# Third mixer cut into slices behind the edge sum of the third graph layer, on one core

## What is computed

```python
xn = _layernorm(x, axis=-1)
x = x + _L3_gnn_ref(xn, ...) + _L3_mix_ref(xn[None], ...)[0]
```

```python
q, k, v = x @ Wq, x @ Wk, x @ Wv           # 8 heads
Q, K = elu(q) + 1, elu(k) + 1
msg = Q (K^T v) / (Q sum(K))                # per head
msg = _layernorm(msg @ Wm, g1, b1)
h = relu(concatenate([x, msg], axis=-1) @ W1) @ W2
return x + _layernorm(h, g2, b2)
```

## Time and profile before

| | us |
|---|---|
| median of the 3 runs | 9672.11 |
| the profiled execution: its time | 9659.98 |
| the profiled execution: its span | 9658.3 |
| third graph layer, 6966 to 8807 | 1841 |
| in it, the stage of `state_scan`, 7468 to 8327 | 859 |
| third mixer, 8807 to 9190 | 383 |

### The profile page before, as it was taken

One profiled execution on the slowest core, in us unless ns is written; L12 is line 12 of the kernel. 1 busy time (PEld: TensorE's weight loads), 2 busy tenths in 40 slices (PEclk: granted clock), 3 DMA queues, 4 the chain that ended last, 5 costly groups with the idle time before them and its releaser, 6 DMA issues. The chain is left out here.

```text
span 9658.3 us, 89308 instructions
## 1 busy us (share of the span) xinstructions
PE 6492.2 (67%) x25974; PEld 4040.2 (42%) x25974; DVE 5133.1 (53%) x10543; ACT 2741.6 (28%) x6163; POOL 3646.3 (38%) x3646
## 2 busy tenths in 40 slices
PE   6848587799577556479965645655843777547766
PEld 6824233344455434347743333433441333223344
DVE  7832475323788654621067555455664888543221
ACT  0112100222355133112224432331233555233311
POOL 2635577001277367230054745750120555110111
PEclk5569656899799766679987776656976999768878
DMA  4200233010377333125433324320030222200022
GB/s 110 71 6 11 60 104 100 31 40 20 107 204 204 91 111 103 38 74 171 146 96 97 103 73 136 102 68 3 25 115 20 78 68 68 80 20 4 8 77 73
DMA packets 440397, 752.07 MB, mean 78 GB/s; under 512 B 172541, under 2 KB 268763, under 8 KB 437489
## 3 DMA queue, kind: packets, MB, share of 16 engines
q0 software_dynamic: 182080, 437.26, 16.5%
q1 hardware_dynamic: 239699, 288.90, 9.3%
q10 hardware_dynamic: 18136, 20.19, 0.6%
HBM read 666.38 MB, written 79.35 MB: 77 GB/s over the span
## 5 line engine op out<-in xcount | busy, mean ns | idle before, releaser
L2619 POOL DMA_INDIRECT R<-table,edges x1248 | 1228.2, 984 | 602.9 <-issue 299.8
L2671 DVE TENSOR_TENSOR acc<-acc,PS 125x256 f32 (+3 forms) x1664 | 705.5, 424 | 772.5 <-PE PS L2688 656.7
L2688 PE MATMUL PS<-R,hot 128*125 128x256 f32 (+1 forms) x1664 | 799.5, 611 | 244.8 <-ACT R L2631 72.7
L2688 PEld LDWEIGHTS PS<-R,hot 128*125 128x125 f32 x1664 | 400.9, 281 | 642.5 <-DMA R<-table,edges 253.9
L2631 ACT ACTIVATE R<-R,TW 128x128 f32<-128x128 f32 (+1 forms) x1248 | 493.6, 431 | 552.1 <-DMA R<-table,edges 549.7
L2437 PE MATMUL PS<-S,hotT 125*128 125x100 bf16 (+1 forms) x6240 | 352.8, 214 | 417.5 <-DVE hotT L2544 403.9
L2619 POOL DMA_INDIRECT xx<-table,edges x416 | 417.8, 1004 | 362.8 <-PE PS L2688 292.0
L1918 POOL DMA_INDIRECT sorted_edges<-edge_rows,edge_place x391 | 401.7, 1027 | 323.3 <-DVE edge_place L2156 114.0
L2686 PE MATMUL PS<-R,hot 128*125 128x258 f32 x1664 | 411.3, 398 | 140.3 <-DVE acc L2669 128.4
L2437 PEld LDWEIGHTS PS<-S,hotT 125*128 125x128 bf16 x6240 | 302.3, 110 | 468.6 <-DVE hotT L2544 377.7
L2619 POOL DMA_INDIRECT room<-table,edges x416 | 407.4, 979 | 239.3 <-PE PS L2688 147.2
(11 more groups left out here) (739 smaller groups left out, 13581.5 us busy)
## 6 DMA issues: line engine op xcount, KB each, us to landing
rowb<-slo_row SPq DMA_DIRECT2D x260, 250.0 KB
W<-in_L_ffn_W1p SPq DMA_DIRECT2D x32, 1024.0 KB
W<-in_L_ffn_W2p SPq DMA_DIRECT2D x32, 1024.0 KB
near<-dst_row SPq DMA_DIRECT2D x98, 256.0 KB
R<-table,edges POOLq DMA_INDIRECT x1248, 2.8
W<-in_L_ffn_w SPq DMA_DIRECT2D x16, 1024.0 KB
hib<-hi_mask SPq DMA_DIRECT2D x260, 50.0 KB, 9.8
g<-gate_rows POOLq DMA_DIRECT2D x8, 1568.0 KB
```

The source lines that it names most:

```text
L2619: pool.indirect_dma_start(self.R[:, u, 0:self.W], None, self.table[:, :], bass.IndirectOffsetOnAxis(ap=self.G.edges[:, g, 0:1], axis=0)).t ...
L2671: v.tensor_tensor(to, to, self.G.PS[0:P, self.bank + k, 0:self.WH], ALU.add).then_inc(self.put, 1)
L2688: mm = pe.matmul(self.G.PS[0:P, self.bank + k, 0:self.WH], hot, self.R[:, u, :], start=True, stop=True)
```

## The change

`gnn3` runs the edge sum in `aggregate`, before the state-space part, with an accumulator and 16 slots of its own, two heads on ACT and two on DVE, PSUM banks 5 to 7; 16 gathers are issued already in `edge_weights`. The mixer is written again as a class `Mix3` with a generator for each of PE, ACT and DVE. Each generator gives 110 slices, and each engine takes one behind every batch of four tiles, the last six at the end. Slices by number: q 8, keys and values 27, attention 7, Wm 7, first norm 9, feed-forward 42, second norm 10. `state_scan` loses the edge sum. `x` and normed `x` stay in `G.xx`, so nothing is parked or fetched back; the graph branch's local result is stored before the state-space part, in a block that waits for its landing. `mix3` is gone.

```diff
@@ third mixer @@
+class NormSlices:
...
+    def tensor(self, pe, u):
...
+            for k in range(KD):
+                mm = pe.matmul(PS[:, u % 2, 0:CW], G.mean[:, :], self.x[:, k, ts(u, CW)], ...)
+            mm.then_inc(self.mean_done, 1)
...
+            pe.wait_ge(self.squared, i + 1)
...
+            mm.then_inc(self.var_done, 1)
+    def scalar(self, act, u):
+        x, i = self.x, u - 1
+        if 0 <= i < NCH:
+            act.wait_ge(self.var_done, i + 1)
...
+            act.activation(self.root[i % 2][:, :], ..., ACT.Ln, bias=self.G.eps[:, 0:1]).then_inc(self.log_done, 1)
+            act.wait_ge(self.log_done, i + 1)
+            act.activation(self.root[i % 2][:, :], ..., ACT.Exp, scale=-0.5).then_inc(self.rooted, 1)
+        if u < NCH:
+            act.wait_ge(self.centred, u + 1)
...
+            act.activation(self.sq[u % 2][:, :, :], x[:, :, ts(u, CW)], ACT.Square).then_inc(self.squared, 1)
...
+                ins = act.activation(x[:, k, ts(i, CW)], ..., ACT.Identity, scale=..., bias=...)
+class Mix3:
...
+    def scalar(self, act):
+        for i in range(NCH):
+            act.wait_ge(self.q_low, i + 1)
+            act.activation(self.two[i % 2], self.two[i % 2], ACT.Exp).then_inc(self.q_exp, 1)
+            yield
+        yield
+        for t in range(T):
+            act.wait_ge(self.kv_low, t + 1)
+            act.activation(self.low[t % self.RS], ..., ACT.Exp).then_inc(self.kv_exp, 1)
+            yield
...
+        for i in range(NCH):
+            act.wait_ge(self.at_mm, i + 1)
...
+            act.activation(self.two[i % 2], PS[:, 0:KD, 0:CW], ACT.Ln, bias=self.G.tiny[:, 0:1]).then_inc(self.at_ln, 1)
+            act.wait_ge(self.at_ln, i + 1)
+            act.activation(self.two[i % 2], self.two[i % 2], ACT.Exp, scale=-1.0).then_inc(self.at_inv, 1)
+            yield
...
+        for i in range(NCH):
+            def relu(m):
+                act.wait_ge(self.up, i * MH + m + 1)
...
+                act.activation(self.hid[m], PS[:, m % 2, 0:CW], ACT.Relu).then_inc(self.hidden, 1)
+            for half in (0, 2):
+                relu(half)
+                yield
+                relu(half + 1)
+                yield
+                yield
@@ def aggregate(nc, G, sums, early=0, own=None, ranking=None, mixer=None): @@
             @block.scalar
             def _(act):
-                for g in range(ET):
-                    sums.scalar(act, g)
+                slices = mixer.scalar(act) if mixer else iter(())
+                for b in range(NB):
+                    for j in range(TB):
+                        sums.scalar(act, b * TB + j)
+                    next(slices, None)
+                for _ in slices:
+                    pass
...
             @block.tensor
...
+                for b in range(NB):
+                    for j in range(TB):
+                        sums.tensor(pe, b * TB + j)
+                    next(slices, None)
@@ def state_scan @@
-                    for g in range(m * TB, m * TB + TB) if m < NB else []:
-                        sums.scalar(act, g)
...
-                    for g in range((m - 1) * TB, m * TB) if 1 <= m <= NB else []:
-                        sums.tensor(pe, g)
@@ def gnn3 @@
-        table_rows(nc, G, G.xn, KD, ..., park=((G.kept[0], flat3(G.xT)), (G.kept[1], flat3(G.xn))), norm_of=G.xT)
-        edge_weights(nc, G, AL, H, TW, False, True, None)
...
+            acc = s1.sb("acc", [P, T, W + H])
+            sums = EdgeSums(G, s1, table, W, H, TW, acc, 16, bank=5, banks=3)
+            table_rows(nc, G, G.xn, KD, p("gat_w_T"), W, table, G.wa[4], H, AL, acc=acc, norm_of=G.xT)
+            edge_weights(nc, G, AL, H, TW, False, True, sums)
+            with Stage(nc) as s2:
+                aggregate(nc, G, sums, sums.early, mixer=Mix3(G, s2, I))
+            settle(nc, G, acc, W, H, p("gat_b"), 1e-16)
...
+                    sp.dma_start(G.kept, flat3(local)).then_inc(restored, 16)
+                    sp.wait_ge(restored, 16)
```

More of the change, by code:

```diff
@@ L2689, in tensor, with aggregate @@
         mm.then_inc(self.summed, 1)
-def aggregate(nc, G, sums, early=0, own=None, ranking=None):
+def aggregate(nc, G, sums, early=0, own=None, ranking=None, mixer=None):
     NB = ET // TB
@@ L2703, in _ @@
                     ranking.sync(sp)
+                if mixer:
+                    mixer.sync(sp)
                 if own is not None:
@@ L2714, in _ @@
             def _(act):
-                for g in range(ET):
-                    sums.scalar(act, g)
+                slices = mixer.scalar(act) if mixer else iter(())
[5 more added lines that the diff above has]
+                    pass
             @block.vector
             def _(v):
+                slices = mixer.vector(v) if mixer else iter(())
                 if ranking:
@@ L2736, in _ @@
                         ranking.step(v, (b - 8) // 3)
+                    next(slices, None)
                 if ranking:
                     ranking.finish(v)
+                for _ in slices:
+                    pass
             @block.tensor
             def _(pe):
+                slices = mixer.tensor(pe) if mixer else iter(())
                 if ranking:
                     ranking.tensor(pe)
-                for g in range(ET):
-                    sums.tensor(pe, g)
+                for b in range(NB):
+                    for j in range(TB):
+                        sums.tensor(pe, b * TB + j)
+                    next(slices, None)
+                for _ in slices:
+                    pass
 def table_rows(nc, G, src, kc, w, W, table, wa=None, H=0, AL=None, mul=None, acc=None, park=(), norm_of=None):
@@ L3199, in state_scan @@
         PS = G.PS
-        sums, acc_clear, NB = make_sums(s), s.sem("acc_clear"), ET // TB
         with nc.Block() as block:
[L3202 to L3206, removed]
             @block.sync
@@ L3320, in _ @@
                     read_out(m)
[L3321 to L3329, removed]
                 finish(NCH - 1)
@@ L3368, in gnn3, with _ @@
         restored = s.sem("restored")
-        AL, TW = s.sb("AL", [P, T, 2 * H]), s.sb("TW", [128, ET, H])
-        table_rows(nc, G, G.xn, KD, p("gat_w_T"), W, table, G.wa[4], H, AL, park=((G.kept[0], flat3(G.xT)), (G.kept[1], flat3(G.xn))), norm_of=G.xT)
-        edge_weights(nc, G, AL, H, TW, False, True, None)
-        def beside(stage):
-            return EdgeSums(G, stage, table, W, H, TW, acc, 20, room, bank=6, banks=2, split=1)
+        with Stage(nc) as s1:
+            AL, TW = s1.sb("AL", [P, T, 2 * H]), s1.sb("TW", [128, ET, H])
+            acc = s1.sb("acc", [P, T, W + H])
[5 more added lines that the diff above has]
+            settle(nc, G, acc, W, H, p("gat_b"), 1e-16)
+            local = s1.sb("local", [128, KD, NC])
+            rows_to_cols(nc, G, acc[:, :, 0:D], D, local)
+            with nc.Block() as block:
+                @block.sync
+                def _(sp):
+                    sp.dma_start(G.kept, flat3(local)).then_inc(restored, 16)
+                    sp.wait_ge(restored, 16)
         with Stage(nc) as s2:
@@ L3392, in gnn3 @@
             softplus_cols(nc, G, dt)
[L3393 to L3401, removed]
-                    sp.dma_start(flat3(G.xT), G.kept[0]).then_inc(restored, 16)
+            state_scan(nc, G, xc, dt, X, z, p("A_log"), G.vec("L3_gnn_D_param"), S, xc)
             dense_cols(nc, G, xc, KD, p("out_proj_w_T"), KD, z)
             finish(nc, G, z, far)
-            with Stage(nc) as s3:
-                s3.sem("all_back")
-                with nc.Block() as block:
-                    @block.sync
-                    def _(sp):
-                        sp.wait_ge(restored, 48)
         hl, ha, g = [s.sb(x, [128, KD, NC]) for x in ("hl", "ha", "g")]
@@ L3498, in build @@
                 gnn0(nc, G, I)
-            elif k in MIX:
+            elif k in GNN:
                 GNN[k](nc, G, I)
-                MIX[k](nc, G, I)
+                if k in MIX:
+                    MIX[k](nc, G, I)
             if k == 1:
```

286 lines of the change are left out of this document (257 added, 29 removed).

## The result

| | before | after |
|---|---|---|
| median of 20 runs each | 9676.87 | 9696.25 |
| ratio, 95% interval | | 1.0022 [1.0014, 1.0029] |
| profiled execution, its span | 9658.3 | 9684.9 |
| edge sum's stage with mixer (before: mixer alone, 383) | | 805 |
| scan's stage (before with the edge sum in it, 859) | | 491 |

The changed kernel is slower by 0.22%, some 21 us. The ratio leaves out one far slower run of each (14861 and 11885 us, the second at a clock of 0.535). The forecast said slower by 99 us: the direction held, the size was nearly five times too large. The prediction itself put 29 us as what a measurement can tell and gave a result inside that 0.14; this one is inside, and only the 20 runs set it apart from nothing.

The account below looks back on a forecast made before the run. ACT and PE waiting on each other, not POOL's pace, were to bound the new stage. Scan 495 plus stage 870 replace 1242; with small edits of -24, +99 on 9660, and 12 for the median: 9771 us, 8 in 10 within 9650 to 9870.

Parts of the forecast that it names:

- that 0.14: Whole kernel: chance given to a result within 29 us, what a measurement can tell; slower had 0.70, faster 0.16.
- handovers: New edge sum and mixer stage: three of 0.1 us in each of 110 slices add 33 us to 746.
- The lock-step of ACT and PE: New stage: ACT can't scale the next batch until PE finishes its slice, and PE then waits for ACT; feed-forward slices 6.9 us.
- The links: New stage: serial waits per slice between engines, summed over the mixer's parts to 780 us with PE at 2.4 GHz throughout.
- I take 0.85, 30% of the time at 1.2 GHz: 870: New stage: mean granted PE clock 0.85 lengthens 780 us to 870; bounds 815 at 0.94, 935 at 0.76.
- my formula: New stage's time: 1 over (share at 2.4 GHz/780 + share at 1.2 GHz/1186); 0.7 and 0.3 give 870 us.
- The scan alone: Scan's stage without the edge sum: 4.08 us a step, 495 us in place of 859; bounds 485 to 525.
- Small edits: Outside both stages: restore gone -20.5, parking gone -16, local store's block +12, early gathers covered; net -24 us.
- Rival 1: New stage: slices hide behind POOL's 5.0 us per batch, stage about 570, kernel 9471 us; chance 0.15.
- Rival 2: New stage: clock holds at 0.96 and links are shorter, 735 us; stage about 760, 9665 to 9690; chance 0.13.
- Rivals 4 and 5: PE mostly at 1.2 GHz in new stage, 9975 us, chance 0.05; scan steps stay at 5.0 us, 9870, chance 0.04.
- Rival 6: New stage: a drain of 1.38 us behind each table load on the path, +29 us, 9800; chance 0.03.

Follow-up runs that it names:

- cut at ACT: Changed kernel with ACT taking each mixer slice one batch later, behind the next batch's scaling: 9550.04 us, ratio 0.9875 to the kernel before.
- cut at PE: Changed kernel with PE taking its mixer slice ahead of the batch's four products: 9552.35 us, ratio 0.9895 to the kernel before.
- another order: Changed kernel with PE's slice ahead of the products and ACT's slice one batch later: 9536.41 us, ratio 0.987 to the kernel before.

## Why the prediction was right in direction and wrong in size

| stretch | link sum of the prediction | measured | clock |
|---|---|---|---|
| q | 62 | 75 | 0.82 |
| keys and values | 149 | 156 | 0.98 |
| attention | 72 | 80 | 0.80 |
| Wm | 51 | 53 | 0.94 |
| first norm | 87 | 105 | 0.73 |
| feed-forward | 263 | 266 | 1.00 |
| second norm | 62 | 70 | 0.81 |
| sum | 746 (780 with handovers) | 805 | 0.90 |

- **The lock-step of ACT and PE: right,** and shown from four sides: cut at ACT (-158 us of stage), cut at PE (-154), scaling taken out of it (-130), scaling made longer (+102). The feed-forward slice was forecast at 6.9 and lasted 6.69.
- **The links, 780 us: some 25 too large.** Without the some 50 us that the traces put down to the low clock, 805 leaves 755. It shows where the clock was 1.00: the feed-forward has 263 and 13 of handovers in the sum and took 266. That 780 lies within 3% of the measured 805 is luck, since the one is meant at the full clock and the other has the low clock's cost in it.
- **The step that failed: "I take 0.85, 30% of the time at 1.2 GHz: 870".** It charged 90 us for the clock, and the slices show some 50. Its price was "the slice takes 3.0 more and the last pair 0.9 more", 3.9 us for a batch at 1.2 GHz. The 24 slow slices took 1.3 to 2.8 us more, 2.0 in the mean: the products and at times the first half of the slice ran at the low clock, the second half mostly at the full one (2.35, then 1.67, in the lines above). The level was off too: at the measured 0.90 my formula gives 1 / (0.8/780 + 0.2/1186) = 837, 33 less. And the low clock wasn't spread over the stage: 42 feed-forward slices and the keys and values, 422 of 805 us, had 1.00 and 0.98. I had expected it to fall in most slices of attention and norms, and had that right. Some 40 of the 65 us by which the stage was too dear are the clock's, some 25 the links'.
- **The scan alone, 495: right** (491). Steps last 4.08 as in the tail.
- **Small edits, -24:** restore -20.4 (-20.5), parking -13 (-16), store +9.8 (+12), early gathers hidden. Right.
- **Sum:** 65 of the 68 us by which +99 missed +31 are the stage's term. The range, 9650 to 9870, held the time; the forecast's own, 9715 to 9840, did not. The miss is more than twice what was left of the +99, so the sign came out right with little to spare.
- **The rivals.** Rival 1 (slices hide) did not come, by exactly the order of waits named against it; put in another order it comes, at a stage of 631 rather than 570, since attention and norms keep their own loops. Rival 2 (the clock holds) is nearest to what happened: it named 760 at a clock of 0.96, where 805 and 0.90 were measured, and it deserved more than 0.13. Its "+0" is a slip: 495 + 760 - 1242 - 24 is -11, some 9660. Rivals 4 and 5 fell with 0.90 and 491. Rival 6 fell with the run without table loads.

## What to carry to other kernels

When two streams of work are laced together in order on several engines, find the loop: if engine A's share of stream 1 stands behind its share of stream 2 and that waits for engine B in the same round, the two streams mostly add up (here 106 of the mixer's 382 us were hidden), however idle the engines are. Shift one engine's share by a round (two lines here) and check whether a round falls to the pace of the slowest engine. And price a low TensorE clock where its matmuls are on the path, slice by slice: take the same piece of the loop at either level (here 4.21 and up to 7.0 us) rather than a mean clock over the stage.

## What the runs showed of the hardware that was not expected

- The granted clock stayed at 1.00 through 266 us of feed-forward slices, in which PE was idle for about 55, in pauses of up to 1.6 us in each round. It fell in attention and the first norm, with pauses of 4.4 to 5.8 us between the slice and the next products, and in q with pauses of 3.2. A product's record had a mean of 639 ns in the first norm against 400 in the feed-forward.
- Weight loads slow down with it: 0.33 us, then 0.19 for the same tile size 0.69 later, as do the matmul records beside them (four of 448 columns in 2.35 us, the next four in 1.67). This is the timeline of PE's weight loads in the first norm of the changed kernel.

```profile
7586.42 0.33 PEld L1853 LDWEIGHTS PS<-msg,mean 128*128 128x128 f32 x1 [0.41 <-issue]
7587.11 0.19 PEld L1853 LDWEIGHTS PS<-msg,mean 128*128 128x128 f32 x1 [0.35 <-issue]
```

- Code that is the same in all versions reached the new stage at anything from 7188 to 7203 us in the profiles. So a difference of some 10 us between the times of two single profiles says nothing; the length of a stage, and of single slices in it, can be compared more closely, and the medians of several runs decide on the whole.
